# A third product at full height: the low part of the feed-forward input in both halves of the rows

## The reference, cut to what matters

```
x = x + gelu(x @ mlp_w1 + mlp_b1) @ mlp_w2 + mlp_b2
xm = _ln(x, ln2_g, ln2_b)
logits = xm @ gate_w.T + gate_b
topv, topi = top_k(logits, 2);  gates = softmax(topv)
comb = einsum(gates, one_hot(topi, 4))
for e in range(4):
    he = gelu(xm @ exp_w1[e] + exp_b1[e])
    oe = he @ exp_w2[e] + exp_b2[e]
    moe_out = moe_out + comb[..., e:e + 1] * oe
return x + moe_out
```

## Time and profile before

| | |
|---|---|
| median of 3 runs | 1013.94 us (1009.13 to 1017.40) |
| profiled execution | 1012.27 us |
| its span, first to last instruction | 1010.4 us, 8581 instructions |
| mean granted TensorE clock | 0.772 of 2.4 GHz |
| TensorE, its weight loads | 752.8 us (74%), 449.4 us (44%) |
| VectorE (DVE), ScalarE (ACT), GpSimd (POOL) | 574.3, 306.4, 214.6 us |

### The profile page before, as it was taken

How to read it: one execution, slowest core, us unless ns; L and a number is a source line. 1 busy time by engine, 2 the same in 40 slices (tenths; PEclk the granted TensorE clock), 3 DMA queues, 4 the chain that set the end, 5 groups by cost and what they waited for, 6 DMA issues and landing times. The chain is left out here.

```text
span 1010.4 us, 8581 instructions
## 1 busy us (share of the span) xinstructions
PE 752.8 (74%) x3088; PEld 449.4 (44%) x3088; DVE 574.3 (57%) x942; ACT 306.4 (30%) x571; POOL 214.6 (21%) x184
## 2 busy tenths in 40 slices
PE   2416547773776698968878998968798979897697
PEld 1101114441322465645445565635345647565575
DVE  3669934665599527753896436745995263331300
ACT  0232211133232131652442122552441342451111
POOL 5125511202244101030352101122441011000000
PEclk9996655575778757876899557867899798896679
DMA  6987600048273000371560001462730000000000
GB/s 133 271 210 184 146 8 0 1 66 195 57 182 74 8 1 1 58 192 46 131 146 8 8 0 14 94 151 62 176 74 8 1 1 1 1 1 8 1 1 8
DMA packets 28751, 68.87 MB, mean 68 GB/s; under 512 B 5280, under 2 KB 13104, under 8 KB 28720
## 3 DMA queue, kind: packets, MB, share of 16 engines
q1 hardware_dynamic: 28720, 68.47, 28.9%
HBM read 60.33 MB, written 3.93 MB: 64 GB/s over the span
## 5 line engine op out<-in xcount | busy, mean ns | idle before, releaser
L1539 POOL TENSOR_TENSOR state<-state,C_rows 128x1024 f32<-128x1024 f32 x42 | 113.0, 2690 | 232.7 <-DVE state L1113 232.7
L1113 DVE TENSOR_TENSOR_SCAN state<-decay,dx_rows 128x512 f32<-128x512 f32 x84 | 128.4, 1569 | 26.3 <-PE py L679 18.5
L679 PE MATMUL py<-state,sel 128*96 128x512 f32 x168 | 104.3, 761 | 46.7 <-POOL state L1539 46.7
L1404 ACT ACTIVATE decay<-d_rows,a_neg 128x255 f32<-128x255 f32 x192 | 81.4, 496 | 138.0 <-DMA d_rows<-delta_dram 95.3
L750 PE MATMUL pd<-w_dn,act 128*128 128x192 f32 x480 | 103.7, 377 | 3.4 <-ACT act L1417 3.3
L750 PEld LDWEIGHTS pd<-w_dn,act 128*128 128x128 f32 x480 | 94.4, 224 | 9.0 <-ACT act L1417 4.5
L1106 DVE TENSOR_TENSOR dx_rows<-dx_rows,B_rows 128x1024 f32<-128x1024 f32 x48 | 74.4, 1549 | 20.2 <-DMA dx_rows<-delta_x_dram 20.2
L532 PE MATMUL ps<-hT,w_qkv 64*96 64x256 f32 (+1 forms) x128 | 59.7, 592 | 31.3 <-DVE hT L1258 30.6
L734 PE MATMUL pu<-fT,w_up 128*128 128x256 f32 x180 | 71.5, 484 | 8.4 <-ACT act L1417 7.3
L679 PEld LDWEIGHTS py<-state,sel 128*96 128x96 f32 x168 | 32.0, 207 | 99.0 <-POOL state L1539 58.7
L1417 ACT ACTIVATE act<-pu,b_up 128x256 f32<-128x256 f32 x90 | 37.7, 470 | 100.0 <-PE pu L738 99.8
(11 more groups left out here) (228 smaller groups left out, 1222.5 us busy)
## 6 DMA issues: line engine op xcount, KB each, us to landing
d_rows<-delta_dram SPq DMA_DIRECT2D x48, 512.0 KB, 6.5
dx_rows<-delta_x_dram SPq DMA_DIRECT2D x48, 512.0 KB, 5.1
w_dn<-exp_w_dram SPq DMA_DIRECT2D x1, 2304.0 KB
B_rows<-xdbl SPq DMA_DIRECT2D x4, 512.0 KB, 7.0
C_rows<-xdbl SPq DMA_DIRECT2D x4, 512.0 KB, 10.8
w_up<-exp_w_dram SPq DMA_DIRECT2D x1, 1536.0 KB
delta_dram<-delta SPq DMA_DIRECT2D x4, 384.0 KB, 3.0
delta_x_dram<-delta_x SPq DMA_DIRECT2D x4, 384.0 KB, 3.4
```

The source lines that it names most:

```text
L679: mm = nc.tensor.matmul(py[0:INNER, :], sel[:, first:first + INNER], flat(states[g % held])[:, paths], start=False, stop=(g == GROUPS - 1) ...
L1113: ins = nc.vector.tensor_tensor_scan(flat(states[g % held])[:, both], flat(decay[g % 2])[:, both], dx_rows[g % 2][:, both], 0.0, ALU.mult, ...
L1404: ins = nc.scalar.activation(decay[g % 2][:, k, rest], d_rows[g % 2][:, k, rest], ACT.Exp, scale=a_neg[:, at:at + 1])
L1539: nc.gpsimd.tensor_tensor(now, now, C_rows[:, :], ALU.mult).then_inc(sc_done, 1)
```

## The change

The low part is made for both halves of the rows, `fT_low`, and the third product takes all 128 rows of `w_up_stack` and of `fT_low`. So it also multiplies the low weights by the low input, which the kernel before leaves out. `fT_parts` goes, with the extra copy for the experts' input. The logits take three products for each half of the tokens, `fT`, `fT_high` and `fT_low`; rows 64 to 127 of `w_gate[:, 1]` are zero now (a memset in the opening), and their second load goes. Below the first edit of the diff, line numbers are one lower up to `logits`.

```diff
-        fT_parts = sb("fT_parts", [128, TOKENS], F32R)
+        fT_low = sb("fT_low", [128, TOKENS], F32R)
...
-        b_loads.append((w_gate[64:128, 1, :], t["w_gate"][128:WIDTH, :]))
...
-                for buf in (w_o[0], w_o[1], pad, gn_raw, gn_mv, gn_m):
+                for buf in (w_o[0], w_o[1], w_gate, pad, gn_raw, gn_mv, gn_m):
                     nc.vector.memset(buf[:], 0.0)
...
                             nc.tensor.matmul(out, w_up_stack[:, e, hidden], fT_high[:, :],
                                              start=False, stop=False)
-                            mm = nc.tensor.matmul(out, w_up_stack[64:128, e, hidden], fT_parts[64:128, :],
+                            mm = nc.tensor.matmul(out, w_up_stack[:, e, hidden], fT_low[:, :],
                                                   start=False, stop=True)
...
                             nc.tensor.matmul(out, fT[:, tokens], w_gate[:, 0, :], start=True, stop=False)
-                            mm = nc.tensor.matmul(out, fT_parts[:, tokens].bitcast(F32), w_gate[:, 1, :],
+                            nc.tensor.matmul(out, fT_high[:, tokens].bitcast(F32), w_gate[:, 1, :],
+                                             start=False, stop=False)
+                            mm = nc.tensor.matmul(out, fT_low[:, tokens].bitcast(F32), w_gate[:, 1, :],
                                                   start=False, stop=True)
...
                         nc.vector.tensor_copy(fT[:, :], pu[:, 0:TOKENS])
-                        if i == 1:
-                            nc.vector.tensor_copy(fT_parts[0:64, :], pu[0:64, TOKENS:2 * TOKENS])
-                        nc.vector.tensor_tensor(fT_parts[64:128, :], pu[64:128, TOKENS:2 * TOKENS],
-                                                fT_high[64:128, :].bitcast(F32),
+                        nc.vector.tensor_tensor(fT_low[:, :], pu[:, TOKENS:2 * TOKENS],
+                                                fT_high[:, :].bitcast(F32),
                                                 ALU.subtract).then_inc(mT_done, 1)
```

## The result

| | before | after |
|---|---|---|
| median of 4 runs each, on one chip | 1012.77 us (1009.13 to 1017.40) | 968.04 us (958.89 to 977.95) |
| profiled execution, its span | 1012.27, 1010.4 us | 959.96, 957.9 us |
| mean granted TensorE clock | 0.772 | 0.793 |

The changed kernel is faster: its time is 0.947 of the time before, with a 95% interval of 0.940 to 0.954. The forecast was 971 us. The four runs of the changed kernel form two pairs, 959 and 960, 976 and 978 us, and the ratio goes by the faster pair, to which the profiled execution belongs (by the medians alone it is 0.956).

The account below looks back on a forecast made before the run. TensorE was taken as the bound, busy 752.8 of 1010.4 us. Last block 13.3, mixed blocks 20.6 and clock 7 sum to 41 us: 1012.3 - 41 = 971 us; forecast 963 to 981 (chance 0.60), range 957 to 989.

Parts of the forecast that it names:

- The gap is a change of height, and both go: Each piece: gaps before and behind the 64-row third product vanish, saving 0.39 us at high clock, 0.59 at low.
- Rival 1: Only the gap ahead of the third product goes; the one behind belongs to the type step: 992 us, chance 0.11.
- Rival 4: Full-height load of the third product waits for the product in front, gap stays: slower, 1026 us, chance 0.02.
- 13.3 us for gaps, logits and copy: Last block: 13.8 us from gaps, less 0.86 for extra logits products, plus 0.32 for the dropped copy.
- 4.6 for the clock: Last block, earlier clock rise: 1.5 us on twelve passes, 0.7 on pieces ahead, some 2.4 at the first six pieces.
- the 0.7 taken off for them: Last block: three GELU waits already hid the gap behind a step's last piece, so 0.3 + 0.2 + 0.2 us deducted.
- 0.7 on the pieces ahead: Last block: 0.7 us from an earlier clock rise on the pieces ahead of the twelve L750 passes.
- 20.6 us and 2.4 of clock: Mixed blocks: 6.8 us in each of two scan blocks, 7.0 in the third; clock 0.8 us each.
- the hidden steps and waits of the prediction: Mixed blocks: 5 of 15 steps hidden in each scan block; third block, 13 steps count, 1.2 us for waits.
- Rival 2: Mixed blocks swallow gain waiting for DVE, ACT or POOL; a third of 20.6 us remains: 987 us, chance 0.12.
- The GELU ahead of ACT's decays: Scan blocks: the last GELU before ACT takes up its decays, at 438.43, would come 2.1 us earlier.
- rival 3: Clock rises sooner and more often: 15 us instead of 7, plus 5 where estimates were careful: 958 us, chance 0.13.

Follow-up runs that it names:

- 4-column products: Changed kernel plus one 4-column product in each last-block piece: 991.07 us at rows 64 to 127, 970.93 at 0 to 127, 966.52 at 0 to 95, 987.80 at 0 to 63.
- grouped kernel: Kernel before, with a step's two 64-row third products moved behind both pieces' 128-row products: median 978.13 us, ratio 0.960.
- e2_last_only: Changed kernel with the third product back at rows 64 to 127 in the mixed blocks, full height in the last block only: median 1002.13 us, ratio 0.989.
- edit at L531: L531's second chunk zero-padded from 64 to 128 rows: on the changed kernel 907.43 us, ratio 0.893; on the kernel before 971.38 us, ratio 0.955.

## Why the prediction was right, point by point

**The gap is a change of height, and both go.** Right: 1.27 and 0.67 us a piece, as worked out, and the two rivals on the mechanism fall. The Trainium skill's rule (TensorEngine Tiling (Array Packing), Key Properties: a change of the tiling mode drains the engine) agrees with the runs: the gap stands at each step between 128 and 64 rows that the chains above show. The sizes, 0.2 and 0.3 us, are this case's. Rival 1 (the gap behind belongs to the step of the type) falls by the 4-column products, which pay both gaps inside one type, and by the chain, in which L733 in float32 behind L737 in the rounded type takes 0.43 us. Rival 4 (a full-height load waits for the product ahead) falls by the same rows, 0.12 us for the third product, and by the grouped kernel. The Trainium skill's sentence on row groups that the prediction cited for it (TensorE: Matmul & The Clock Gate, Part 3, The mechanism) does not describe these loads: ahead of the third product's 90 loads in the mixed blocks stood only 3.5 us of idle time, though they take the same rows as the product in front.

**Last block.** 13.3 us for gaps, logits and copy, and 4.6 for the clock were forecast; 20.7 came. The logits cost what was said (L759 and L761, the products with the zero-padded weights, take 0.43 us each twice), and so did the subtraction: 0.41 us on 128 rows, where it was 0.43 on 64.

```profile
L1156 DVE TENSOR_TENSOR fT_low<-pu,fT_high x8: 411/412/414, 348.6 to 911.9; 128x256 fp32r<-128x256 f32 x8
```

The three waits of 0.9 us for GELU are still there, as the 0.7 taken off for them said. So what came beyond the 13.3 is clock, and its places can be named. The first stretch, before and then after, six pieces and the wait behind them:

```profile
920.70:935.60 14.90, 12.52 (x32) 7.49 (x32) 1.28 (x3) 3.80 (x7) 1.46 (x2) 0.54 0.00 0
```

```profile
888.90:899.30 10.40, 8.03 (x33) 6.46 (x33) 1.18 (x3) 3.80 (x7) 1.50 (x2) 0.67 0.00 0
```

4.5 us where the gaps alone give 6 x 0.59 less the 0.3 that the wait hides, 3.2. The down products behind it (935.6 to 946.8 before, 899.3 to 908.9 after) brought another 1.6 from the clock. The four pieces at 922.14 ran in 2.88 us instead of four times 1.87: 4.6, of which 2.4 are gaps, so the term "0.7 on the pieces ahead" was 2.2. The twelve passes brought 1.6, forecast as 1.5 (3.56 less 12 x 0.16 is 1.6 as well; the forecast's 1.5 is a slip of the sum). Together 1.3 + 1.6 + 2.2 + 1.6 = 6.7 of the 7.4 us that came beyond 13.3.

**The mixed blocks.** 20.6 us and 2.4 of clock were forecast, 30.3 came. TensorE's idle time there (span less busy in the block rows) rose by 2.9, 4.9 and 1.0 us, 8.8 together; the hidden steps and waits of the prediction come to 8.8 + 1.7 + 1.2 = 11.7. So hiding was as foreseen in kind and some 3 us smaller. Rival 2 had a rise of 10 us as its sign, and that nearly came; its price did not, for it left a third of 20.6 us and 30.3 arrived. TensorE waits longer where it said: 2.4 us for inv_den in the first mixed block instead of 1.6, 9.8 for hT instead of 9.2, and 4.5 for GELU (L733 in `pu`) instead of 2.4, so that part of a step goes into waits:

```profile
PE ps L531 <- DVE hT L1257: 9.8, 1, 9.8
PE pu L733 <- ACT act L1416: 4.5, 4, 1.8
```

The overlap with the scores has gone too; a product of 48 rows that started together with L738 now comes 0.21 us behind L737:

```profile
395.30 0.28 PE L737 MATMUL pu<-fT_low,w_up_stack 128*128 128x256 f32 x1
395.51 0.50 PE L850 MATMUL ps<-k_stack,q_stack 48*128 48x128 f32 x4
```

But the clock in these blocks was sized at 0.8 us each, and that is the term that was furthest off. In the first mixed block, from the first piece of the second step to the end of 24 down passes, before and after:

```profile
365.20:384.80 19.60, 18.67 (x61) 13.39 (x60) 6.30 (x14) 4.55 (x9) 0.00 (x0) 0.56 0.00 1
```

```profile
361.80:374.30 12.50, 11.57 (x62) 9.40 (x60) 5.06 (x12) 4.20 (x8) 0.00 (x0) 0.91 0.01 1
```

7.1 us in one stretch with four pieces, whose gaps are worth 4 x 0.59 = 2.4 at most: with dense pieces the clock rose with the second, before 365 us, and held through the products behind. The GELU ahead of ACT's decays came 10.8 us earlier, counted from the block's start, and not 2.1, so the scan moved with it instead of absorbing it.

In the third mixed block it went the other way. The first run of L532 took 7.6 us at a clock of 0.89 in the kernel before, and that of L531 took 12.5 at 0.50 in the one after, though nothing about it was changed:

```profile
776.70:784.30 7.60, 7.60 (x25) 3.43 (x24) 3.20 (x7) 1.88 (x4) 0.99 (x1) 0.89 0.00 0
```

```profile
750.90:763.40 12.50, 12.50 (x25) 5.14 (x24) 3.10 (x7) 1.88 (x4) 1.00 (x1) 0.50 0.00 0
```

That took 5 us back at once, and the block gained 6.3 instead of 7.8. In all six executions of this code the run took 12.5 us; of before there is only one. Against `e2_last_only`, whose third mixed block has 64-row products and a run of 12.5 us as well, it gained 10.4 (150.6 to 140.2).

**The sum.** Gaps and logits come out as forecast where they can be read bare. The profiled execution gained some 10 us more than forecast (52.5 - 41, with 1.5 ahead of the mixed blocks); at most 3 of them are hiding, so the clock, taken as 7 us with bounds of 0 and 15, was worth some 14 to 17. That is rival 3, which had 0.13: its 958 us is close to the faster pair of runs (959 and 960), though the clock rose only behind the fourth piece after the experts' turn. How much of it an execution gets varies: in three of the six executions with this code the first mixed block took 210 us, and with that the gain would be about 42. That the median, 968.04, fell so close to 971 is luck in part: it lies midway between the two pairs of runs. What stays open is what decides whether the clock rises at the start of that first run of L531; no experiment tried it, other than by filling its gaps, after which it always rose.

## What to carry to other kernels

Read the weight loads for idle time without a releaser: where products of 64 rows alternate with ones of 128, each step between them costs 0.2 us at the high clock and 0.3 at the low one here, more than the whole rounded product of 256 columns (0.12 and 0.21). Pad the short operand with zeros or with something useful to 128 rows, or put the short products behind one another; the rows themselves cost nothing here. (96 rows were tried only with a product of 4 columns.) Where the clock often stands at its lower level, expect more than the sum of the gaps: in this kernel the clock rose once they were filled, and the edit at L531 gained 49 us where its gaps were put at 18 to 28.

## What the runs showed that was not expected

- 96 rows behave as 128: the last block took 76.5 us with the 96-row product and 76.6 with the 128-row one, 93.1 with 64 rows at either end. The Trainium skill (TensorEngine Tiling (Array Packing), Available Configurations) lists row modes of 128, 64 and 32 alone, and the runs agree: a product of 96 rows between two of 128 pays no gap, so 96 rows are no mode of their own.
- A product of 4 columns costs 0.11 us at the high clock and 0.21 at the low one between products of its own height, and nothing beside the two gaps at another.
- The same 24 records, which alternate in height, take 7.0 or 12.5 us from execution to execution by the clock alone, and with what follows this spreads the first mixed block by 10 us; once they are of one height, no run took more than 7.4 us in 16.
- DVE's subtraction from PSUM over 128 rows takes 0.412 us, and 0.427 over 64.
